# Two eight-expert layers: every expert over every token, or tokens sorted by expert through DRAM

## The chip, the cores and the metric

The kernel runs on one core of one Trainium2 chip. The metric is device time in microseconds (us) of one execution; lower is better. Everything is float32 unless said otherwise.

## The reference, cut to what matters

Sixty-four sequences of 64 tokens, 128 values each, go through twelve residual layers: cross-attentions to a context of 128 tokens a sequence, a gated recurrence, low-rank and four-expert layers, softmax attentions, a convolutional state-space layer. Two of the twelve send each token to one of eight experts, and these are what the change rewrites:

```python
# layer L2 (called m2 in the kernel): x + routed(layernorm(x))
idx = argmax(softmax(x @ Wr + br)); gate = max(softmax(...))
# tokens past an expert's capacity (4096 / 8 = 512, counted over the whole batch) are dropped
h = relu(expert_in @ W1[e] + b1[e]);  out = gate * (h @ W2[e] + b2[e])
# layer L3 (called m3): no gate, no capacity
idx = argmax(softmax(xf @ Wg + bg))
h = gelu(x @ W1[e] + b1[e]);  out = h @ W2[e] + b2[e]     # for e = idx of the token
```

W1[e] and W2[e] are 128 x 128.

## The kernel before

The 64 sequences are worked in four passes. In a pass two slots, 0 and 1, each hold 8 sequences: 512 tokens as four tiles of 128 (`TILES` = 4). One slot in one pass is called a unit here; there are eight. Each slot has its own buffers (X, Z, A, T, big, P, small, ...) and its own four banks of PSUM (`ps_0`, `ps_1`, 512 float32 columns a bank). So a unit goes through all layers as one chain, and the two slots are independent streams that fill each other's gaps on each engine.

For each engine there is a generator `program(s)` that yields between steps ("beats"); `weave` merges the two slots' generators by a bit string in `ORDER` that was written beforehand: one bit a beat says which slot comes next. Each engine then runs its instructions strictly in that order, and an instruction that waits holds back everything behind it on its engine, the other slot's too. There is one such order each for TensorE (pe, 2,498 beats), ScalarE (act), VectorE (dve), GpSimd (pool) and the DMA queue of SyncE (sp). On DVE, `link` puts a semaphore between dependent instructions of one chain.

The stages of a unit, in order, by the names used below: three groups of attention heads (`h0`, `h1`, later `h2`; 44 TensorE beats each, in four pairs j0 to j3), `rnn`, `lora`, `x1` (cross), `lin`, `m1` (softmax attention and the four-expert layer), `h2`, `loc` (softmax attention), `m2`, `x3` (concat), `ssm`, `m3`, then the next pass.

In m2 and m3 every one of the eight experts is computed for all 512 tokens and a mask makes the wrong ones vanish. A unit and layer takes on TensorE:

- `turn_onehot`: four transposes of the one-hot choice; ScalarE copies the rows, scaled so that a wrong expert gets -1e30, into `mTb` (L1212, L1213);
- `up` (L889): 8 matmuls of 512 columns with W1[e]; `mask` (L893): 8 bf16 matmuls of 512 columns that add the -1e30 into the same bank, so that relu or gelu gives 0 for wrong tokens; ScalarE's `hidden` (L1315) evicts with bias and function;
- `down`: 8 x 4 matmuls of 128 columns with W2[e] (recorded at the helper `tokens`, L486), all summed in one bank; `tokens8` (L908): 4 matmuls that add the second bias.
- In m2 also a transpose of the scaled tokens, and `positions`-like matmuls (L921 to L926) that count tokens by expert for the capacity.

A float32 matmul leaves two records in the trace, a transpose or a bf16 matmul one. All weights stay in SBUF (`wts`); the first-layer weights of both expert layers are centred once at the start (`centre_weights`, L693, 9 chunks), which makes the mean subtraction of the layer norm unnecessary.

Of the kernel before, what the change touches and what calls it, by code (L numbers as in the profile page):

```python
# [13 lines left out]
D = 128  # L14
BATCH, SEQ, CTX = 64, 64, 128
SLOTS = 2
# [16 lines left out]
EXPERTS = 8  # L33
CAPACITY = BATCH * SEQ // EXPERTS
# [8 lines left out]
           ("bqkv", 3), ("moe2_b1", 8), ("conv_w", 8), ("conv_b", 2), ("moe3_b1", 8),  # L43
# [4 lines left out]
           ("loc_q", 128), ("loc_k", 128), ("loc_v", 128), ("moe2_r", 8), ("moe2_w1", 1024), ("x3a", 128), ("ssm_in", 512),  # L48
           ("moe3_r", 8), ("moe3_w1", 1024)]
# [5 lines left out]

CONSTS = [("ident", 128), ("center", 128), ("hmask8", 8), ("cos", SEQ), ("sin", SEQ),
          ("causal_add", SEQ), ("causal_T", SEQ), ("upto", 128), ("iota", 16)]


def offsets(table):  # L60
    at, out = 0, {}
    for name, n in table:
# [14 lines left out]
    pe=(2498, int(""  # L77
        "404600c8640004010800000000069ebffdf375f56bac10c1af4ddee629cc55cb06914148810afbdc018a1ca1dd3aea84c3e9"
        "c718588ed73ea800018bfd2ff8eeff53ec40001008e1d720e74051814070f83ff8382011c3a86cb5fd6febfbbc1c3fc3f6be"
        "cccfc9476f7fbd7dee707114148a0a7def5401651c3ac0c754163eb71c58b2c5ae72000031bf767ff15fde3dc4a0c3e0ebb8"  # L80
        "2246bffffc0003902b06a40100000e439f3ff8b6fd6eeffdff647fc30abfa6ee58a2955ed703911029140530ef3d502c48e0"
        "ebaea85bfff7b7be0b144aacd402003e97fd1f15d1f4000129ddea1b801158affffe1a82e00e20000000896b8ff7faeb75f5"
        "ffc1860ae9bffefeffc1f85bf2f38ca502505053d3ced401660e33f2d482affffffffe07ffbdffffeefc192d91eeb2a04181"
        "2dfb1ff19e1d41389fff30f", 16)),
    act=(1741, int(""
        "4120206080200000c00039bbffe4faf4fbbecfa82c43130cc0901c000424af78f68bde1856031e6e0e18fee19bfff5810301"
        "4e974e32054b018c306405ee0ccfddff73fffee99f10e8fbf7be8b0cc090382010ab95a0f687de350c30cdaa00f1fecc9bff"
        "dd21ccbfaed022dbf00068fb40010001773393fdefffde7fefeef1a24256470cc024118020224f0efcd3fffb35f0081ed507"
        "0fa7f80df9800ecf5fc310055f1e58ff000000009cf3e7bbf67ffbb7ff5ff13e03e6e06c0840e02010cb62fe641bffffff5f"
        "ff4ffff5838af0bfd2213de037fa0178ff", 16)),  # L90
    dve=(2030, int(""
        "1001238a8c0040200000001bbf6bbd7c3b15a5ce31825da73db18614c0dbf16c50d0df8007c68ea4daee65bf0c38303288d8"
        "f8abf796e6dedd83ec028a69e0c7641de80000620488fb961e400a5ff9c78fe3e7186a7f643cfffe78f03cfc5b1593fc3b50"
        "11d294e78078efc30e483c818de81af7e6bb6d5be17ffde6e068e5c64002b6561230800007c0206d7baeef7bfc1ff1e25d73"
        "35cc61923a0f3f0e858d060ee1da28cca539dcddf97fa33c066518c2fd7aeee06d941ef377981c01973e306dc5801800000e"
        "370022eddcb9ffc441aa4fffeb5fe9e1ce79e037d928b46fc3e5011e88ce7b1913fbffffe1fffcffffe4f1b19c78c77f000e"
        "b367fd", 16)),
    pool=(610, int(""
        "6c5018df30532b53182161b93a2fbb7378c7904c253ac34fc0ff53185609d43957dee378c7cb219c0e0dee3a2b53142131b5"
        "3af57f8db607c0b9807706bc935fa660ac0ae49ffff3be7d1d", 16)),  # L100
    sp=(26, int(""
        "1333335", 16)))


def weave(program, order):
# [50 lines left out]
def build(nc, x, ctxin, ctok_in, fold, cols, weights, consts, out):  # L156
# [4 lines left out]
    with stack:  # L161
# [113 lines left out]
        def block_of(h, n):  # L275
            return (h % 2) * (n // 2) + h // 2
# [1882 lines left out]
```

## Time and profile before

| | |
|---|---|
| time, median of 3 runs | 2491.32 us (2490.16 to 2494.02) |
| span of the profiled execution (first to last instruction) | 2495.5 us |
| busy share of the span | TensorE 94%, weight loads 63%, VectorE 59%, ScalarE 47%, GpSimd 37% |
| DMA | 26.57 MB, nearly all of it in the first of 40 slices of the span |
| mean granted TensorE clock | 0.989 of full speed |

The span of the one profiled execution is 4.2 us above the median of the runs. PE is TensorE, PEld its weight loads (which overlap with matmuls), DVE VectorE, ACT ScalarE, POOL GpSimd, SP SyncE. L486 is line 486 of the kernel. In a group, "busy" is the time in which at least one of its instructions ran, so that busy divided by the count is the price of one in a packed stream, while the mean of one is longer, since matmuls overlap.

### The profile page before, as it was taken

Reading aid. Unit: us, or ns where it says so; the run is one execution under the profiler, and the core shown is the slowest. Engines: PE = TensorE matmul, PEld = TensorE weight load, DVE = VectorE, ACT = ScalarE, POOL = GpSimd, SP = SyncE. Lnnn points to the kernel's source line nnn. Section 1 sums busy time; section 2 is a strip of 40 time slices with the busy share of each in tenths; the row PEclk is TensorE's granted clock in tenths of the full one; section 3 lists DMA queues with packets and bytes.
Section 4 is the critical chain, followed back from the end, with each engine's and each line's share of the span. In section 5 each row is a group of like instructions: output and inputs, shape, how many; then the busy total and the mean of one; then the engine's idle time right before and its main releaser. Section 6 shows DMA issues by size and latency. Waiting matters only on the chain.

```text
span 2495.5 us, 41931 instructions
## 1 busy us (share of the span) xinstructions
PE 2349.7 (94%) x16426; PEld 1565.0 (63%) x16426; DVE 1479.9 (59%) x4040; ACT 1180.3 (47%) x2996; POOL 929.6 (37%) x853
## 2 busy tenths in 40 slices
PE   9999989999999999999999999999999999999998
PEld 6665656666766665666666665566566666656665
DVE  5357556665475566666564567665565555664653
ACT  5454334455444534545554444445454444354543
POOL 5235343433233335434231344443322343544410
PEclk9999989999999999999999999999999999999999
DMA  5000000000000000000000000000000000000000
GB/s 233 1 1 1 1 10 9 10 1 18 1 1 10 1 1 10 10 9 9 9 1 9 1 1 9 1 10 9 13 1 1 5 1 1 1 1 1 2 1 9
DMA packets 6821, 26.57 MB, mean 11 GB/s; under 512 B 864, under 2 KB 992, under 8 KB 5984
## 3 DMA queue, kind: packets, MB, share of 16 engines
q1 hardware_dynamic: 6624, 23.89, 2.7%
q8 instruction: 130, 2.13, 0.4%
q14 instruction: 67, 0.55, 0.1%
HBM read 21.79 MB, written 2.10 MB: 10 GB/s over the span
## 4 chain that ended last, share of the span: by engine, by line
PE 71%; DVE 18%; POOL 4%; ACT 4%; issue 3%; DMA 0%; DVEq 0%; POOLq 0%; ACTq 0%
PE ps L486 10%; PE ps L499 6%; PE ps L549 6%; PE ps L518 6%; PE ps L889 4%; PE ps L510 3%; PE ps L628 3%; PE ps L471 3%; PE ps L603 3%; PE ps L596 3%; PE ps L650 3%; PE ps L836 2%; PE ps L601 2%; PE ps L846 2%; PE ps L677 2%
## 5 line engine op out<-in xcount | busy, mean ns | idle before, releaser
L1919 POOL TENSOR_TENSOR P<-P,small 128x384 f32<-128x384 f32 x384 | 317.7, 850 | 555.2 <-DVE small L1430 554.8
L1140 ACT ACTIVATE P<-ps,small 128x192 f32<-128x192 f32 x768 | 314.2, 421 | 147.1 <-DVE small L1422 145.6
L1892 POOL TENSOR_TENSOR small<-small,mhalf 128x4 f32<-128x4 f32 x112 | 128.4, 1147 | 543.4 <-DVE small L1410 272.1
L499 PE MATMUL ps<-kvT,big 128*128 128x192 f32 x1536 | 313.8, 334 | 7.2 <-DVE big L1437 2.8
L499 PEld LDWEIGHTS ps<-kvT,big 128*128 128x128 f32 x1536 | 248.2, 190 | 91.2 <-issue 53.5
L1422 DVE TENSOR_REDUCE small<-ps 128x2 f32<-128x384 f32 x384 | 210.1, 551 | 107.7 <-PE ps L499 100.8
L486 PEld LDWEIGHTS ps<-wts,P 128*128 128x128 f32 x1920 | 231.5, 192 | 43.8 <-issue 30.0
L486 PE MATMUL ps<-wts,P 128*128 128x128 f32 x1920 | 249.0, 279 | 5.2 <-POOL P L2009 2.6
L2009 POOL TENSOR_TENSOR P<-T 128x512 f32<-128x512 f32 x96 | 126.6, 1319 | 206.7 <-ACT T L1289 107.6
L518 PEld LDWEIGHTS ps<-value,big 128*128 128x128 f32 x1536 | 178.1, 192 | 26.9 <-issue 20.7
L518 PE MATMUL ps<-value,big 128*128 128x128 f32 x1536 | 188.4, 277 | 0.5 <-DVE big L1462 0.5
L510 PE MATMUL ps<-cst,P 128*128 128x128 f32 x1152 | 167.3, 279 | 18.8 <-POOL P L1919 9.3
L549 PE MATMUL ps<-kvT,score 128*128 128x512 f32 x384 | 177.9, 604 | 4.6 <-ACT kvT L1115 3.5
L510 PEld LDWEIGHTS ps<-cst,P 128*128 128x128 f32 x1152 | 132.7, 143 | 51.1 <-issue 18.2
L1140 ACT ACTIVATION_READ_ACCUMULATOR P<-ps,small 128x1 f32 x768 | 156.8, 204 | 0.0
L1315 ACT ACTIVATE P<-ps,col 128x512 f32<-128x512 f32 x128 | 81.4, 684 | 134.5 <-PE ps L893 134.3
L1488 DVE SCALAR_TENSOR_TENSOR X<-ps,small,X 128x128 f32<-128x128 f32 x256 | 71.9, 343 | 104.4 <-PE ps L486 100.1
L372 POOL TENSOR_TENSOR big<-big,cst 128x1024 f32<-128x1024 f32 x48 | 106.6, 2222 | 66.1 <-ACT big L1307 37.8
L628 PEld LDWEIGHTS ps<-Vbd,P 128*64 128x64 f32 x3072 | 99.0, 139 | 51.1 <-issue 34.4
L1627 DVE TENSOR_REDUCE small<-ps 128x8 f32<-128x512 f32 x128 | 87.7, 685 | 59.3 <-PE ps L650 59.1
L1157 ACT ACTIVATE big<-ps 128x512 f32<-128x512 f32 x96 | 57.3, 596 | 135.1 <-PE ps L510 134.7
L549 PEld LDWEIGHTS ps<-kvT,score 128*128 128x128 f32 x384 | 69.5, 192 | 81.3 <-issue 72.6
(288 smaller groups left out, 4483.5 us busy)
## 6 DMA issues: line engine op xcount, KB each, us to landing
ctok<-ctok_dram SPq DMA_DIRECT2D x8, 512.0 KB, 3.7
ctxT<-ctx_dram SPq DMA_DIRECT2D x8, 512.0 KB, 3.9
wts<-weights_dram SPq DMA_DIRECT2D x1, 2530.0 KB, 23.7
wts<-weights_dram SPq DMA_DIRECT2D x1, 2189.0 KB, 18.1
X<-x_dram SPq DMA_DIRECT2D x8, 256.0 KB, 3.0
big<-fold_dram SPq DMA_DIRECT2D x2, 1024.0 KB, 7.9
out_dram<-X SPq DMA_DIRECT2D x8, 256.0 KB, 2.0
wts<-weights_dram SPq DMA_DIRECT2D x1, 1536.0 KB, 26.1
```

What stands on the lines that cost most here:

```text
L372: return engine.tensor_tensor(big[s][:, 1024 * (t % 2):1024 * (t % 2) + 1024].rearrange("p (b j t) -> p b j t", b=2, t=SEQ), src[:, 128 * ...
L486: m = pe.matmul(part(s, k, t), tile_of(src, t), w, start=first and t == 0 and c == 0, stop=last and t == TILES - 1 and c == len(pairs) - 1)
L499: m = pe.matmul(ps[s][:, at:at + KEYS], big[s][:, BANK * b + 128 * p:BANK * b + 128 * p + 128], kvT[s][:, keys_at(b):keys_at(b) + KEYS], s ...
L510: m = pe.transpose(part(s, k, p), probs(s, j)[:, PAIR * p + at:PAIR * p + at + 128], C("ident"))
L518: m = pe.matmul(part(s, 1, t), big[s][:, 1024 * t + 128 * k:1024 * t + 128 * k + 128], value[:, at:at + 128], start=(t == 0 and k == 0), s ...
L549: m = pe.matmul(bank(s, qp_bank(g, r) + k), score[:, 128 * block_of(h, nh):128 * block_of(h, nh) + 128], latents(s), start=True, stop=True)
L628: m = pe.matmul(ps[s][64 * bb:64 * bb + 64, at:at + 18], src(bb, j), Vbd[s][:, 18 * (8 * b + j):18 * (8 * b + j) + 18], start=True, stop=True)
L1140: m = act.activation(probs(s, b // 2)[:, to:to + KEYS], ps[s][:, at:at + KEYS], ACT.Exp, bias=small[s][:, 4 * e + p:4 * e + p + 1], accum_ ...
L1422: dve.tensor_reduce(small[s][:, at:at + 2], ps[s][:, BANK * k:BANK * k + 2 * KEYS].rearrange("p (c k) -> p c k", k=KEYS), AX.X, ALU.max, n ...
L1892: pool.tensor_tensor(rstd(s, name, n), variance(s, name, n), mhalf[:, 0:n], ALU.pow).then_inc(*sig("rstd", s))
L1919: m = pool.tensor_tensor(view, view, over(small[s][:, at:at + 2], 2, [128, 2, KEYS]), ALU.mult)
L2009: pool.tensor_tensor(P[s][:, 1024 + 512 * (k % 2):1536 + 512 * (k % 2)], tmp(s, k % 2), tmp(s, 2 + k % 2), ALU.mult)\
```

## The change

In both layers the 512 tokens of a unit are sorted by expert and each expert works on its own tokens only.

1. DVE's new `places` computes from the counts, for each token, a row in a table of 11 tiles of 128 rows (`ROUTED` = 4 + 8 - 1; each expert's tokens begin on a new tile), and for each of the 11 tiles its expert (`which`). m3 now makes the same counting matmuls as m2.
2. GpSimd scatters the tokens by four indirect DMAs (one for 128 rows of 512 bytes) to `x_sorted` in DRAM. SyncE's queue reads the 11 expert numbers into a register one by one, loads for each tile its expert's weights (128 x 385 float32: W1, W2, b2 broadcast, b1; 197 KB) from a table in DRAM, and then reads the sorted tokens in three DMAs, for groups of 4, 4 and 3 tiles.
3. TensorE transposes 11 tiles, ACT copies them, TensorE makes 11 `up` matmuls of 128 columns, ACT evicts 11 times 128 columns with bias and function, TensorE makes 11 `down` matmuls, DVE adds b2 group by group.
4. SyncE writes the three groups to `y_sorted` in DRAM, GpSimd gathers back by four indirect DMAs, DVE adds to the residual.

The expert weights leave `wts`, so their centring goes as well (9 chunks become 5), and DVE's `centre` is put in for m2 and m3. At the start SyncE also fills `x_sorted` with two copies in DRAM. Semaphores that both slots shared (`ONCE`) become one per slot, mostly on the counters of a stream (`tok`, `zT`, `n_proj`, `pl`), at the same waits. The orders are new: pe has 2,294 beats.

```diff
+                def routed(s, i, layer):                     # SyncE
+                    for g, (first, tiles) in enumerate(GROUPS):
+                        yield
+                        sp.wait_ge(*on("tok", s, i, ROUTES[layer] + ".e"))
+                        for k in range(first, first + tiles):
+                            e = sp.value_load(which[s][0:1, k:k + 1], min_val=0, max_val=128 * (EXPERTS - 1))
+                            sp.dma_start(expert(s, k), table[layer][bass.ds(e, 128), :]).then_inc(experts_in[s][g], 16)
+                    yield
+                    sp.wait_ge(moved[s], 128 * n + 64)
+                    for g in range(3):
+                        sp.dma_start(by_tile(sorted_x(s, g)), rows_in(x_sorted[s], g)).then_inc(sorted_in[s][g], 16)
+                    for g in range(3):
+                        yield
+                        sp.wait_ge(*on("tok", s, i, f"{ROUTES[layer]}.y{g}"))
+                        sp.dma_start(rows_in(y_sorted[s], g), by_tile(sorted_y(s, g))).then_inc(sorted_out[s], 16)
...
-                def up(s, layer, e, src, first):
-                def mask(s, e, first):
-                def down(s, i, layer, e):
...
+                def routed(s, i, layer):                     # TensorE
+                    def turn_x(g):
+                        pe.wait_ge(sorted_in[s][g], 16 * n + 16)
...
+                    def up(g):
+                        pe.wait_ge(experts_in[s][g], 16 * tiles * (n + 1))
+                        pe.wait_ge(*on("zT", s, i, f"{ROUTES[layer]}.t{g}"))
...
+                            m = pe.matmul(part(s, U_BANK[g], k), expert(s, first + k)[:, 0:128], tile_of(sorted_xT(s, g), k),
+                                          start=True, stop=True)
...
+                    yield from turn_x(0)
+                    yield from turn_x(1)
+                    yield from up(0)
+                    yield from turn_x(2)
+                    yield from up(1)
+                    yield from down(0)
+                    yield from up(2)
+                    yield from down(1)
+                    yield from down(2)
...
+                def places(s):                               # VectorE, 11 steps, 7 of them before "which" is out
...
+                def scatter(s, i, layer):                    # GpSimd
+                    pool.wait_ge(*on("tok", s, i, ROUTES[layer] + ".d"))
+                    for t in range(TILES):
+                        pool.indirect_dma_start(x_sorted[s], bass.IndirectOffsetOnAxis(ap=dest[s][:, t:t + 1], axis=0), tile_of(N[s], t), None)\
+                            .then_inc(moved[s], 16)
+                def gather(s, i, layer):
+                    pool.wait_ge(sorted_out[s], 48 * (2 * i + layer) + 48)
...
+                    dve.wait_ge(moved[s], 128 * (2 * i) + 128)
```

## Rows read from the trace of the kernel before

**Rows 1.** The page: busy time by engine, and granted clock in 40 slices
```profile
PE 2349.7 (94%) x16426; PEld 1565.0 (63%) x16426; DVE 1479.9 (59%) x4040; ACT 1180.3 (47%) x2996; POOL 929.6 (37%) x853
...
PEclk9999989999999999999999999999999999999999
```

**Rows 2.** Waits of TensorE: waited for, us in total, times, longest
```profile
PE ps L471 <- DVE P L1405: 31.1, 42, 2.9
```

**Rows 3.** The page: the chain that ended last, by engine
```profile
PE 71%; DVE 18%; POOL 4%; ACT 4%; issue 3%; DMA 0%; DVEq 0%; POOLq 0%; ACTq 0%
```

**Rows 4.** Groups by line, TensorE: busy us, mean ns, idle before them
```profile
L486 PE MATMUL ps<-wts,P 128*128 128x128 f32 x1920 | 249.0, 279 | 5.2 <-POOL P L2009 2.6 <-DVE P L1827 1.9 <-DVE X L1488 0.5
...
L510 PE MATMUL ps<-cst,P 128*128 128x128 f32 x1152 | 167.3, 279 | 18.8 <-POOL P L1919 9.3 <-ACT big L1157 3.1 <-issue 1.9
...
L889 PE MATMUL ps<-Z,wts 128*128 128x512 f32 x128 | 64.6, 629 | 0.3 <-ACT P L1315 0.3
L889 PE MATMUL ps<-A,wts 128*128 128x512 f32 x128 | 62.2, 609 | 2.3 <-ACT P L1315 1.3 <-ACT A L1115 0.9
L471 PE MATMUL ps<-cst,P 128*128 128x128 f32 x352 | 58.6, 291 | 35.8 <-DVE P L1405 31.1 <-DVE P L1782 4.5
...
L893 PE MATMUL ps<-mTb,pick_b 8*128 8x512 bf16 x128 | 24.6, 384 | 0.9 <-ACT T L1213 0.9
...
L908 PE MATMUL ps<-wts,T 8*128 8x128 f32 x128 | 17.0, 271 | 0.0
...
L478 PE MATMUL ps<-cst,small 128*8 128x128 f32 x64 | 10.1, 283 | 0.0
...
L693 PE MATMUL ps<-wts,cst 128*128 128x512 f32 (+1 forms) x18 | 7.7, 571 | 0.0
...
L923 PE MATMUL ps<-ohb,upto_b 128*128 128x8 bf16 x32 | 3.2, 168 | 0.5 <-DVE ohb L1768 0.5
```

**Rows 5.** Stretches: length, busy PE, PEld, DVE, ACT, POOL, clock, DMA share, GB/s
```profile
10.00:20.00 10.00, 9.90 (x61) 5.65 (x60) 5.65 (x16) 3.42 (x7) 6.27 (x4) 1.00 1.04 422
...
70.00:120.00 50.00, 49.08 (x244) 32.33 (x243) 19.51 (x38) 24.96 (x83) 15.04 (x18) 1.00 0.00 1
...
590.00:600.00 10.00, 7.77 (x47) 4.86 (x47) 6.16 (x13) 6.47 (x22) 6.95 (x6) 0.83 0.00 0
2340.00:2370.00 30.00, 26.04 (x348) 18.27 (x347) 22.67 (x47) 15.80 (x29) 8.82 (x5) 1.00 0.01 2
2376.00:2496.00 120.00, 104.52 (x648) 68.81 (x648) 51.71 (x196) 44.55 (x73) 9.89 (x14) 0.97 0.02 5
2432.00:2448.00 16.00, 9.71 (x48) 5.77 (x48) 12.45 (x34) 5.27 (x8) 3.85 (x6) 1.00 0.00 1
```

**Rows 6.** Timeline of VectorE in m2, last pass: start, length
```profile
2381.70 0.19 DVE L1778 SCALAR_TENSOR_TENSOR small<-small 128x32 f32<-128x32 f32 x1
```

**Rows 7.** Groups by line, ScalarE
```profile
L1315 ACT ACTIVATE P<-ps,col 128x512 f32<-128x512 f32 x128 | 81.4, 684 | 134.5 <-PE ps L893 134.3
...
L1115 ACT ACTIVATE Z<-ps 128x512 f32<-128x512 f32 x72 | 43.0, 598 | 50.5 <-PE ps L471 50.2
...
L1263 ACT ACTIVATE P<-ps,small 128x128 f32<-128x128 f32 x32 | 11.3, 367 | 7.3 <-DVE small L1593 7.2
```

**Rows 8.** Groups by line, GpSimd
```profile
L1892 POOL TENSOR_TENSOR small<-small,mhalf 128x4 f32<-128x4 f32 x112 | 128.4, 1147 | 543.4 <-DVE small L1410 272.1 <-DVE small L1512 167.6 <-DVE small L1728 36.3
...
L372 POOL TENSOR_TENSOR big<-big,cst 128x1024 f32<-128x1024 f32 x48 | 106.6, 2222 | 66.1 <-ACT big L1307 37.8 <-PE ps L650 25.3 <-DVE big L1682 2.5
```

**Rows 9.** DMA issues: size of one, median us to landing
```profile
X<-x_dram SPq DMA_DIRECT2D x8, 256.0 KB, 3.0
...
out_dram<-X SPq DMA_DIRECT2D x8, 256.0 KB, 2.0
```

**Rows 10.** Groups by line, VectorE: two instructions of one shape
```profile
L1405 DVE TENSOR_TENSOR P<-X,small 128x512 f32<-128x512 f32 x48 | 48.4, 1009 | 21.3 <-POOL small L1892 21.0
...
L1782 DVE TENSOR_TENSOR P<-X,small 128x512 f32<-128x512 f32 x8 | 5.5, 692 | 0.3
```

More of the change, by code:

```diff
@@ L445, in _ @@
                     sp.dma_start(wts[:, cut[k]:cut[k + 1]], weights[:, cut[k]:cut[k + 1]]).then_inc(w_main, 16)
+                for s in range(SLOTS):
+                    sp.dma_start(x_sorted[s].rearrange("(k p) d -> p k d", p=128), by_tile(x[:, 0:128 * ROUTED])).then_inc(filled, 16)
                 weave(program, ORDER["sp"])
@@ L1553, in top2_weights, with routed @@
+                def routed(s, i, layer):
+                    for g in range(3):
+                        yield
+                        dve.wait_ge(*on("y_ps", s, i, f"{ROUTES[layer]}.y{g}"))
+                        dve.tensor_tensor(by_tile(sorted_y(s, g)), by_tile(bank(s, D_BANK[g])[:, 0:128 * GROUPS[g][1]]), expert_b2(s, g),
+                                          ALU.add).then_inc(*sig("tok", s))
                 def top2_weights(s, i, name, e):
@@ L1785, in moe2 @@
                         yield from contexts(s, i)
+                    yield from routed(s, i, 0)
                     yield
-                    dve.wait_ge(*on("y_ps", s, i, "m2"))
-                    link(add_scaled(s, i, 2, lambda t: small[s][:, DN + 12 + t:DN + 13 + t]))
+                    dve.wait_ge(moved[s], 128 * (2 * i) + 128)
+                    for t in range(TILES):
+                        at = small[s][:, DN + 12 + t:DN + 13 + t]
+                        m = dve.scalar_tensor_tensor(tile_of(res(s, i), t), tile_of(N[s], t), at, tile_of(res(s, i), t), ALU.mult, ALU.add)
+                    link(m)
                 def concat(s, i):
@@ L1937, in kv_context @@
                     if i >= 0:
[L1938 removed]
+                        pool.wait_ge(*on("tok", s, i, "ssm.g"))
                     else:
@@ L2028, in program @@
                         yield from inverse_root(s, i, "m2")
+                        yield from scatter(s, i, 0)
                         if i < PASSES - 1:
@@ L2031, in program @@
                             yield from inverse_root(s, i, "ctx1")
+                        yield from gather(s, i, 0)
                         yield from inverse_root(s, i, "x3")
@@ L2043, in program @@
                             yield from inverse_root(s, i, "x0")
+                        yield from gather(s, i, 1)
+                        if i < PASSES - 1:
                             yield from kv_latents(s, i)
@@ L2067, in rows_of @@
         return w.reshape(n, 128, -1).transpose(1, 0, 2).reshape(128, -1)
-    def at(p, a):
-        out = np.zeros((128, a.shape[-1]), np.float32)
-        out[:p] = a
-        return out
     def per_partition(v, n):
```

510 lines of the change are left out of this document (275 added, 235 removed), and 2 rows, old and new, of the table WEIGHTS.

## The prediction, as it was put on record

> **What bounds the kernel now.** I read the page first: TensorE is busy for 2349.7 us of a span of 2495.5 us, in every slice of it, at a granted clock of 0.9 and more of 2.4 GHz [rows 1]. So 145.8 us are all the idle time that TensorE has. The chain that ended last agrees: 71% of it is TensorE, and no DMA is in it [rows 3]. Then the waits: the largest for which TensorE stood is a transpose behind a layer norm, 31.1 us in 42 times, never over 2.9 us [rows 2]. No engine is waited for long; the two slots fill each other's gaps. Hence two questions decide: how much TensorE work goes, and how much idle time comes in because a unit now waits in each expert layer for DMAs that take work of no engine.
>
> **What TensorE loses and gains** (eight units, two layers each; a float32 matmul is two records). Prices are busy time by count [rows 4].
> - Removed: `up` 64.6 + 62.2 = 126.8 us; `mask` 24.6; `down` 8 x 4 x 2 x 16 = 1024 of the 1920 records of L486 at 249.0 / 1920 = 0.130 us, 132.8; the bias matmuls L908 17.0; the one-hot transposes L478 10.1; the token transpose of m2, 32 of the 352 of L471 at 0.166, 5.3. Sum 316.6 us.
> - Added: 11 x 16 = 176 transposes at 167.3 / 1152 = 0.145 us, 25.5; `up` 11 x 2 x 16 = 352 records of 128 columns at 0.130, 45.7; `down` the same, 45.7; in m3 14 counting matmuls of 8 columns a unit, 112 at 3.2 / 32 = 0.10, 11.2. Sum 128.1 us.
> - Centring: 18 records become 10, 8/18 of 7.7 us = 3.4 us less.
>
> Net -191.9 us: TensorE 2349.7 - 191.9 = 2157.8 us. With the idle time of today that is 2303.6 us of span. I take the group prices as they are, since weight loads overlap in the new matmuls as in L486's.
>
> **The other engines** don't become the bound. ACT loses 81.4 us (L1315) and six small copies a unit, and gains 176 evictions of 128 columns at 0.367 us = 65 us and 48 copies at up to 0.6 = 29 us [rows 7]: about even. DVE gains, per unit, two `places` of 11 steps at 0.2 us [rows 6], six additions of up to 0.69 us and two centrings of 0.7 to 1.0 us [rows 10], some 10 us, 80 in all: 1560 us, two thirds of the new span. POOL gains 16 x 8 = 128 indirect DMAs: at 1.1 to 2.2 us (below) 140 to 280 us of its queue beside 930 busy us. The semaphores per slot stand at the same waits as the shared ones, and the instructions behind them are the same: 0. The two fills of `x_sorted` at the start are behind all weights in SP's queue and run while TensorE works: 0; if they were in the way, 0.7 MB each at 422 GB/s [rows 5] is under 4 us. 2.2 MB less of weights could give a few us back only where the start waits for them, and it doesn't: 0.
>
> **The two DMA legs.** The trace of before has no indirect DMA, no register load from SBUF and no wait on DRAM inside a pass. Bounds for one unit and layer:
> - First leg, from the counting matmuls to the first transpose of sorted tokens. `places` 11 x 0.21 = 2.3 us. Four scatters on POOL's queue, each between 1.1 us (its cheapest work on data, four columns) and 2.2 us (its 1024 columns) [rows 8]; I take 1.1, since a scatter handles one number a row: 4.4. Landing 2.0 and reading back 3.0 us, as a store and a load of 256 KB [rows 9]. Sum 11.7 us, with 2.2 us each 16.1. Beside it SP loads 11 experts, 2.17 MB, 5.1 us at 422 GB/s [rows 5], and reads 11 numbers first, which may cost 0 or up to 1.1 us each; the three reads of tokens stand behind all of this in the same queue. From `which`, 1.6 us in, at 11 x 0.8 = 9 us and the reads of 3, plus some of the data still under way: 14 to 17. I take 16 us for the leg.
> - Second leg: last b2 addition 0.5, store 2.0, four gathers 4.4, landing 2.5, additions to the residual 1.4 (four of 0.34): 10.8, at 2.2 us a gather 15. I take 12 us.
> - Between them the experts' own chain (transposes, copy, `up`, evictions, `down`) is 6 to 8 us.
>
> Who covers a leg? The bits of the new pe order can be decoded by counting beats. Slot 0 in m2 waits behind slot 1's h2: 2 projections, 4 score beats and 8 beats of j0 (two passes), or 15 beats (one): 13 to 16 us of TensorE work. One slot alone in such heads keeps TensorE at 98%: from 70 to 120 us slot 0's h1 runs with hardly any work of slot 1, and PE is busy 49.08 of 50 us [rows 5]. The second leg of m2 has 16 beats of heads, 17 us. There the legs cost nothing. Weak covers:
> - Last pass. From slot 0's count in m2 on, today's end is 2376 to 2496: 120 us, PE busy 104.5, idle 15.5 [rows 5]. Four expert layers lie there, each 191.9 / 16 = 12 us lighter; 11 beats of loc (some 15 us) move in as cover: 104.5 - 48 + 15 = 71 us of work. The new chain of slot 1: 24 us behind slot 0, leg 16, experts 6, leg 12, x3 and ssm to m3's logits 38 (as in today's), routing 4, leg 16, experts 8, leg 12, add 1: 137 us. Idle 66, so +50 us.
> - Slot 0's m3 stands behind 10 beats of loc in two passes and 5 in the third; a stretch of such work has PE at 26.04 of 30 us [rows 5]: 3 + 3 + 8 = 14 us. Its second leg has some 8 us of cover for 12, three times, since the next pass's h0 waits for the residual: +12. Slot 1 in the first pass has 6 beats of rnn and lora (PE at 9.71 of 16 in a comparable stretch [rows 5]: +6) and then 3 beats of x1: +7. Together +39, say 40.
> - Where the cover is 13.4 us and the leg 16, five or six times: +15.
>
> Added idle 105 us. Sum: 2303.6 + 105 = 2408.6 us of span; the median of runs lies 4.2 us under today's span, so **2404 us**. Today's PE-only idle after a wait already drops the clock (590 to 600: 2.2 us idle, clock 0.83 [rows 5]); longer gaps could cost some us more in the tail, and I let the bounds hold that.
>
> **A rule that speaks against this change.** In today's trace two VectorE instructions of one shape take 692 ns in one place and 1009 ns on average in another [rows 10], so something holds DVE up beside POOL's work. The Trainium skill, "SBUF — State Buffer", section "Who interferes with whom", says that a VectorE copy or tensor_scalar in a two-port mode fully blocks GpSimd's descriptor writing, and names a software DMA that took 620 ns alone and about 3100 ns beside a copy. By that rule a scatter or gather that meets such an instruction would be some 2.5 us later, and all eight of a layer 20 us later at worst. It is the mechanism of the third rival. The skill's "DMA: Bandwidth & Descriptors", section on the anatomy of a SWDGE DMA, gives 2.0 us plus bytes / 436e3 for one: 2.15 us for 64 KB, as an estimate, and with it the legs would be as above.
>
> **Rivals.**
> 1. Everything but the tail is hidden, because the order was laid for legs of just this length: 2303.6 + 50 - 4.2 = 2349 us. For it: today's waits are all under 3 us [rows 2]. Against: the covers of 5 loc beats and of 3 x1 beats are too thin by count. Chance 0.15.
> 2. The legs are 3 to 5 us longer a layer than I have them (gathers at 2.2 us, reads behind 11 loads). In an order fixed beforehand TensorE stands for each: 16 x 3 to 16 x 5, so 2452 to 2484 us. Chance 0.10.
> 3. The other side: POOL's queue or SP's is far dearer, 10 us a layer. TensorE stands at the sorted tokens, and the gather, in order in POOL's queue, holds back the other slot's normalising (L1919), for which its transposes wait. 2404 + 160 = 2564 us. It decides from (2496 - 2404) / 16 = 5.8 us a layer on. For it: nothing in the trace bounds an indirect DMA or 11 register loads from above. Against: 5.8 us a layer is 0.7 us on every one of eight indirect DMAs beyond 1.1, with all slack gone. Chance 0.16.
> 4. The cut buys nothing because the units' chains, not TensorE, set the time: gain and loss cancel within 5 us. At 94% busy that needs 190 us of new idle time. Chance 0.04.
>
> My forecast has 0.55, with a range of its own of 2350 to 2450 us.
>
> **How the numbers follow.** 0.2% of this time, 5 us, is about what a measurement can tell from no change. Faster: forecast, rivals 1 and 2, 0.80; same 0.04; slower 0.16. The range leaves out rival 3 and a little below rival 1: 2325 to 2495 us holds about 0.8.
>
> **What would show it.** PE busy near 2158 us, L889's and L893's groups gone, two new groups of 352 records near 46 us each: the sum is right. Waits of TensorE for sorted tokens (a DMA) few and under 5 us, except in the last 140 us and at slot 0's m3: the covers are right. TensorE waits of 6 us and more in every layer, on a DMA or behind L1919, would make the prediction wrong upwards; a last stretch shorter than 137 us, downwards. PE busy well over 2158 us would mean that the prices of records, or the clock, are not today's.

## The result, and the profile after

The changed kernel took 2553.4 us (median of 4 runs, 2543.2 to 2556.6) against 2492.7 us before in the same session: ratio 1.0231, 95% interval 1.0204 to 1.0258. It is 61 us slower: the forecast of 2404 us and its range of 2325 to 2495 us were wrong, and so was the sign.

The page of the changed kernel: span, busy time by engine, granted clock, the chain that ended last.

```profile
span 2554.8 us, 42262 instructions
...
PE 2247.1 (88%) x15778; PEld 1542.7 (60%) x15778; DVE 1560.1 (61%) x4270; ACT 1126.7 (44%) x3032; POOL 1048.8 (41%) x981
...
PEclk9999999988989998998899999999699999999866
...
PE 61%; DVE 20%; issue 5%; SPq 5%; POOL 4%; ACT 4%; DMA 3%; POOLq 0%; DVEq 0%; ACTq 0%
```

Against [rows 1] TensorE lost 103 us of busy time, where 192 were forecast, and its idle time went from 146 to 308 us, where 251 were forecast. The clock shows 8, and once 6, where a pass is in its expert layers (one 8, at 960 to 1020 us, lies outside them), and 6 at the end. TensorE's share of the chain that ended last fell from 71% [rows 3] to 61%, and SyncE's queue (SPq) and DMAs are now in it. (The kernel before read its data less early than the table ahead of the prediction says: its first slice moved 233 GB/s for 62 us, some 14.5 of the 26.57 MB. The DMAs were in no wait of note there.) Waits of TensorE (us in total, times, longest):

```profile
PE ps L531 <- DVE P L1450: 46.4, 36, 4.6
PE ps L960 <- DMA P<-x_sorted: 32.7, 18, 7.2
PE ps L944 <- DVE ohb L1592: 29.4, 12, 8.0
PE ps L538 <- DVE big L1547: 17.0, 7, 5.5
```

The first is the wait of [rows 2], grown from 31.1 us. The new waits for sorted tokens (a DMA) are just 33 us; those on VectorE grew more. All waits together are 290 us against 137, 189 of them on VectorE against 90. The groups that the forecast had priced (busy, mean ns, idle before):

```profile
L960 PE MATMUL ps<-cst,P 128*128 128x128 f32 x176 | 35.6, 338 | 32.9 <-DMA P<-x_sorted 32.7
L971 PE MATMUL ps<-Z,big 128*128 128x128 f32 x128 | 22.3, 331 | 1.8 <-ACT Z L1351 1.8
L971 PE MATMUL ps<-A,big 128*128 128x128 f32 x128 | 18.4, 291 | 0.0
L971 PE MATMUL ps<-T,held 128*128 128x128 f32 x96 | 13.3, 275 | 0.0
```

The transposes cost 35.6 us (forecast 25.5), `up` 22.3 + 18.4 + 13.3 = 54.0 (forecast 45.7): 40% and 18% over the forecast. Work that nobody touched got dearer too: the matmuls of the scores (L601 here, L549 in the kernel before) take 191.0 us, where the same 384 records took 177.9.

Where the time lies is seen in stretches that begin when slot 0's counting matmuls run in m2 (length, busy PE, PEld, DVE, ACT, POOL, clock, DMA share, GB/s). The changed kernel: its first stretch of expert layers, the stretch behind it, and the last one:

```profile
472.00:764.00 292.00, 241.39 (x1454) 169.50 (x1456) 178.81 (x519) 126.89 (x358) 116.64 (x118) 0.89 0.22 63
764.00:1100.00 336.00, 318.46 (x2442) 214.46 (x2442) 212.72 (x539) 152.35 (x396) 145.62 (x123) 0.96 0.02 5
...
2388.00:2555.00 167.00, 94.47 (x628) 69.30 (x628) 80.14 (x268) 43.62 (x97) 45.47 (x47) 0.68 0.37 105
```

The kernel before, its first stretch of expert layers:

```profile
470.00:760.00 290.00, 274.69 (x1682) 185.80 (x1681) 169.06 (x487) 146.32 (x366) 97.55 (x96) 0.99 0.02 6
```

TensorE is busy 33 us less there, and the stretch is 2 us longer. The last stretch grew from 120 us [rows 5] to 167, at a clock of 0.68. Below is one layer's first leg as it stands on the chain that ended last (start, length in us), from the last step of `places` ahead of `which` to the first transpose, with the eleven expert loads between.

```profile
602.69 0.18 DVE which L1618
602.89 0.28 SPq L440
603.19 0.15 SPq L440
603.60 0.36 SPq L441
604.01 0.27 SPq L440
...
615.02 0.34 SPq L441
615.41 0.43 SPq L445
615.88 4.09 DMA P<-x_sorted
620.02 1.11 PE ps L960 x4
```

A register load of an expert's number (L440) and its DMA's issue (L441) repeat every 1.13 us, 12.5 us for eleven, and the reads of the tokens (L445) stand behind them. From the one-hot choice at 600.17 (the counting matmuls follow at 600.4) to 620.02 the leg is 20 us, where 16 were forecast. GpSimd was done with the last of the four scatters at 611.5, 3.9 us before the reads were issued.

### The profile page after: what moved, and what is told of

It reads as the page before. It is cut to its first block, busy times and chain, and to the rows that moved or that the text cites. A ratio compares the mean times of both kernels' runs of the same rounds, so it can differ in the third digit from the quotient of the medians.

```text
span 2554.8 us, 42262 instructions
## 1 busy us (share of the span) xinstructions
PE 2247.1 (88%) x15778; PEld 1542.7 (60%) x15778; DVE 1560.1 (61%) x4270; ACT 1126.7 (44%) x3032; POOL 1048.8 (41%) x981
## 4 chain that ended last, share of the span: by engine, by line
PE 61%; DVE 20%; issue 5%; SPq 5%; POOL 4%; ACT 4%; DMA 3%; POOLq 0%; DVEq 0%; ACTq 0%
PE ps L551 7%; PE ps L570 6%; PE ps L538 5%; PE ps L601 4%; PE ps L562 4%; PE ps L680 3%; PE ps L655 3%; PE ps L898 3%; PE ps L653 3%; PE ps L648 3%; PE ps L531 2%; PE ps L888 2%; SPq L440 2%; DVE small L1435 2%; PE ps L702 2%
## 5 line engine op out<-in xcount | busy, mean ns | idle before, releaser
L601 PE MATMUL ps<-kvT,score 128*128 128x512 f32 x384 | 191.0, 641 | 3.3 <-DVE big L1482 1.7
L538 PEld LDWEIGHTS ps<-wts,P 128*128 128x128 f32 x896 | 117.0, 199 | 44.3 <-issue 27.0
L680 PEld LDWEIGHTS ps<-Vbd,P 128*64 128x64 f32 x3072 | 105.5, 146 | 55.7 <-issue 34.0
L538 PE MATMUL ps<-wts,P 128*128 128x128 f32 x896 | 124.0, 286 | 8.1 <-DVE P L1909 6.3
L601 PEld LDWEIGHTS ps<-kvT,score 128*128 128x128 f32 x384 | 74.7, 206 | 87.5 <-issue 79.6
L680 PE MATMUL ps<-Vbd,P 128*64 128x18 f32 x3072 | 115.9, 218 | 3.2 <-DVE P L1732 2.0
L1159 ACT ACTIVATE Z<-ps 128x512 f32<-128x512 f32 x72 | 43.0, 597 | 152.7 <-PE ps L531 152.5
L1325 ACT ACTIVATE T<-ps 128x512 f32<-128x512 f32 x96 | 57.3, 597 | 119.9 <-PE ps L898 119.7
```

What stands on the lines that cost most here:

```text
L538: m = pe.matmul(part(s, k, t), tile_of(src, t), w, start=first and t == 0 and c == 0, stop=last and t == TILES - 1 and c == len(pairs) - 1)
L601: m = pe.matmul(bank(s, qp_bank(g, r) + k), score[:, 128 * block_of(h, nh):128 * block_of(h, nh) + 128], latents(s), start=True, stop=True)
L680: m = pe.matmul(ps[s][64 * bb:64 * bb + 64, at:at + 18], src(bb, j), Vbd[s][:, 18 * (8 * b + j):18 * (8 * b + j) + 18], start=True, stop=True)
```

## The experiments

The kernel before was run beside each; a ratio is of the runs of one session. x1, s1 and r1 are variants of the kernel before, all others of the changed one. The variants without register loads, those without scatters and gathers, e9 and x1 leave work out, as said at each, and so their output is not the reference's. s1 and s2 change the order alone and don't give the reference's output either; why isn't known, so they are used for their lengths only. Each of the three s runs ran only twice.

```
kernel                                               us     ratio   95% interval
the change                                         2553.4  1.0231  1.0204-1.0258
e1  no register loads                              2525.7  1.0127  1.0096-1.0157
e2  e1, three weight DMAs a layer                  2525.5  1.0133  1.0108-1.0158
e3  no scatters, no gathers                        2541.1  1.0201  1.0173-1.0230
e5  token reads after four expert loads            2537.2  1.0186  1.0148-1.0224
e7  e2 and e3                                      2488.1  0.9983  0.9968-0.9997
n1  e7, token reads ahead of the weights           2484.2  0.9965  0.9942-0.9988
x2  n1, no reads and no stores either              2483.7  0.9966  0.9954-0.9978
x1  the kernel before, 195 us of TensorE cut       2441.9  0.9804  0.9787-0.9822
e4  TensorE filler ahead of two waits a layer      2576.3  1.0350  1.0318-1.0382
e8  expert matmuls twice                           2624.4  1.0509  1.0481-1.0537
e9  places in two constant steps                   2552.0  1.0218  1.0190-1.0245
s1  before, slots apart                            3633.9  1.4560  1.4527-1.4594
s2  the change, slots apart                        3913.2  1.5680  1.5635-1.5724
s3  e7, slots apart                                3659.9  1.4665  1.4630-1.4699
p1  e7 in another order                            2516.7  1.0087  1.0065-1.0109
n2  n1 in another order                            2466.0  0.9882  0.9862-0.9903
r1  before in another order                        2491.6  0.9993  0.9980-1.0005
r2  e5 in another order                            2533.6  1.0152  1.0134-1.0171
```

### The legs: SyncE's queue and the indirect DMAs

e1 takes fixed experts, so nothing is read into registers:

```diff
-e = sp.value_load(which[s][0:1, k:k + 1], min_val=0, max_val=128 * (EXPERTS - 1))
-sp.dma_start(expert(s, k), table[layer][bass.ds(e, 128), :])...
+e = 128 * min(k, EXPERTS - 1)
+sp.dma_start(expert(s, k), table[layer][e:e + 128, :])...
```

> The changed kernel with the 11 expert numbers not read into a register: tile k always loads expert min(k, 7), so most tokens meet a wrong expert; all DMAs keep their size and place. Theory A (SyncE's queue is what the first leg waits for: in the trace of the changed kernel one register load and one DMA issue take 1.13 us together, 11 of them 12.4 us, and the reads of the sorted tokens stand behind them): one load falls to about 0.4 us, the leg shortens by 8 us, of which 5 to 8 reach TensorE in each of 16 layers: 2430 to 2475 us. Theory B (the loss is TensorE's own: gaps behind the router's chain on VectorE, and the clock at half after each gap): only the gaps at the sorted tokens go, 2515 to 2540 us. Theory C (the indirect DMAs on GpSimd and their landing are what is waited for): no change, 2545 to 2560 us.

e2 also loads each group's experts with one DMA:

```diff
-for k in range(first, first + tiles):
-    ... sp.dma_start(expert(s, k), ...)
+e0 = 128 * min(first, EXPERTS - tiles)
+sp.dma_start(held_in..., table[layer][e0:e0 + 128 * tiles, :].rearrange("(k p) c -> p k c", p=128))...
```

> As e1_static, but the weights of a group of tiles come in one DMA, three a layer in place of 11, of the same bytes; the experts are fixed as there. Theory A: the queue work before the reads falls from 12.4 us to some 1.5; the scatter and its landing (9 us after the expert numbers are out) then end the leg, so at most a few us below e1_static, 2400 to 2465 us. If the bytes of the weights (2.17 MB a layer) and not their issue hold the reads back, then equal to the changed kernel, 2545 to 2560 us. Theory B: 2515 to 2540 us. Theory C: 2545 to 2560 us.

e3 leaves out the scatters and gathers (L2046, L2053) on GpSimd:

```diff
-sp.wait_ge(moved[s], 128 * n + 64)
+sp.wait_ge(filled, 32)
+sp.wait_ge(*on("tok", s, i, ROUTES[layer] + ".d"))
...
-dve.wait_ge(moved[s], 128 * (2 * i) + 128)
+dve.wait_ge(sorted_out[s], 96 * i + 48)
```

> The changed kernel without its 128 indirect DMAs: SyncE reads what the start put into the sorted table, VectorE waits for the store of the sorted results and adds its own unsorted tokens; the output leaves the routing out. Register loads, weight loads, reads and stores stay. Theory C: both legs lose their GpSimd part, 4 to 9 us each, 2400 to 2450 us. Theory A: the first leg is SyncE's and stays; only the second shortens by some 6 us, where its cover was thin: 2500 to 2540 us. Theory B: 2530 to 2555 us.

e5 moves the reads up in SyncE's queue:

```diff
 for g, (first, tiles) in enumerate(GROUPS):
+    if g == 1:
+        yield
+        read_tokens(s, n)
     yield
```

> The changed kernel, computing the same, with one edit on SyncE's queue: the three reads of the sorted tokens stand behind the first four weight loads and ahead of the other seven. Theory A (SyncE's queue): the tokens can be there some 14 us after the expert numbers in place of 17 to 19, the weights of groups 1 and 2 some 3 us later than now but still ahead of their matmuls; e1_static, which took 8 us off the queue in each layer, brought 28 us, so some 10 to 15 us: 2535 to 2545 us. Theory D (the two units' own chains and the fixed order set the time, and every leg is only one term): the same range, it doesn't tell them apart. If the reads wait for the scatter at the head of the queue longer than they save: 2555 to 2565 us.

e7 is e2 and e3 together:

> e2_grouped and e3_no_indirect together: no register loads, three weight loads a layer, no indirect DMA; SyncE's reads and stores are all that is left of the legs (some 5 and 3 us in place of 20 and 11). Output without routing. Theory A with C (the legs are the whole loss): 25 us a layer less in the chain, TensorE near its sum of 2158 us plus 150 to 200 us idle: 2330 to 2400 us. Theory D (legs are a part; the rest is the router's chain and places on VectorE, with too little TensorE work left to hide them): 2450 to 2490 us. Theory B (clock): it falls with the gaps, so between.

The register loads are worth 26 us (1.0231 to 1.0127), fewer DMAs nothing more. Theory A expected 78 us and more of e1, so most of the loss isn't there. Reordering the queue, which keeps the function, gets back 11 us, and taking out the indirect DMAs alone 7 us; for these two the intervals overlap with that of the change. On top of e2, taking them out is worth 37 us (1.0133 to 0.9983). That is how two parallel ways of one leg behave: the register loads beside the scatters hide them, and only the longer way counts until it is cut. POOL's two groups in the changed kernel say what one costs:

```profile
L2046 POOL DMA_INDIRECT x_sorted<-P,dest x64 | 65.7, 1026 | 82.1 <-DVE P L1860 44.3 <-DVE dest L1621 22.3 <-issue 15.5
L2053 POOL DMA_INDIRECT P<-y_sorted,dest x64 | 63.7, 995 | 112.0 <-DMA y_sorted<-P 96.7 <-issue 15.3
```

About 1.0 us each, 1.3 with the gap to the next: the forecast's 1.1. Yet with both ways gone e7 stands only 4 us under the kernel before, not 190. In e7 the reads still waited behind 2.2 MB of weights:

```profile
P<-x_sorted SPq DMA_DIRECT2D x32, 256.0 KB, 7.5
```

n1 puts them first (as e5, at `g == 0`); x2 leaves out every way of the tokens through DRAM, the reads and the stores of sorted rows as well:

```diff
-pe.wait_ge(sorted_in[s][g], 16 * n + 16)
+pe.wait_ge(*on("tok", s, i, ROUTES[layer] + ".d"))
```

> The changed kernel without scatters and gathers and with grouped weight loads at fixed experts, as the run at 2488 us, but its three reads of tokens stand ahead of the weight loads in SyncE's queue (tokens are not moved: output is not the reference's). In that run laid apart TensorE still waited 178 us for these reads, 11 us a layer, which landed 7.5 us after their issue behind 2.1 MB of weights. Theory E (a slot's own chain sets the time, the other slot covers most of it): 4 to 6 us less a layer in the chain, of which a quarter reaches the time: 2460 to 2475 us. Rival F (only the written order is wrong, the chain is covered): 2488 us, no change.

> The changed kernel with all ways of the tokens through DRAM taken out of the layer: no scatters, no reads, no stores of the sorted rows, no gathers, and expert weights loaded in three DMAs from fixed experts (TensorE transposes whatever stands in the buffer: output is not the reference's). Places, counting matmuls, copies, additions and the written order stay. Theory H (what still costs 180 us against the sum is the tokens' way out and back): 2350 to 2400 us. Theory G (the order's gaps and the clock, not the DRAM, hold it): 2460 to 2484 us.

Neither moved much: 0.9965 and 0.9966 against e7's 0.9983, with intervals that overlap. n1 stayed above the range of theory E, x2 fell into that of theory G. So all that the legs cost is the way from x2 to the change, 0.9966 to 1.0231, 66 us. And the changed kernel without any leg is within 9 us of the kernel before. In x2 TensorE is busy for 2225.8 us of 2480.2, so it idles for 254 us, 109 more than before the change, though no leg is left, and it is busy for 68 us more than the 2157.8 us of the sum. That refutes the view that the legs ate the gain. Something else had.

### Does cut TensorE work come back?

x1 makes only the cut, in the kernel before: experts 1 to 6 lose their `up` and `down` matmuls, and the masks (which now open their bank's sum), ScalarE's evictions, the waits and the order stay.

```diff
 def up(s, layer, e, src, first):
+    if e not in (0, EXPERTS - 1):
+        return None
...
 def down(s, i, layer, e):
...
+    if e not in (0, EXPERTS - 1):
+        return
```

> The kernel before, with only TensorE's expert work cut: of the eight experts only numbers 0 and 7 keep their up and down matmuls (output is not the reference's); masks, evictions on ScalarE, VectorE's work, waits and order are all kept. That takes 6/8 of 126.8 + 132.8 us, 194.7 us of TensorE's work, as much as my sum gave the whole change, and adds nothing. Theory H (cut TensorE work comes back one for one while the other slot fills its gaps, as the prediction's sum has it): about 2300 us. Theory G (the dense expert matmuls were what filled TensorE while the other slot waited; without them its gaps open and its clock falls): 2380 to 2440 us, waits of TensorE near 220 us.

This is the run that decides: a cut of 195 us, with nothing added, gave 50 us (ratio 0.9804), at the edge of theory G's range. Its page, and its waits of TensorE:

```profile
PE 2232.0 (92%) x15466; PEld 1475.1 (60%) x15466; DVE 1477.4 (61%) x4040; ACT 1178.9 (48%) x2996; POOL 929.3 (38%) x853
...
PEclk9999989998999999989999999999999999999986
```

```profile
PE ps L471 <- DVE P L1409: 44.8, 45, 4.2
PE ps L486 <- ACT P L1319: 13.3, 9, 1.7
PE ps L891 <- ACT P L1319: 11.5, 10, 2.8
```

```profile
L486 PE MATMUL ps<-wts,P 128*128 128x128 f32 x1152 | 165.7, 291 | 19.2 <-ACT P L1319 13.3 <-DVE P L1831 2.7 <-POOL P L2013 2.6
```

TensorE's busy time fell by 118 us, not by 195. In the two groups that were cut, L486 lost 768 records and 83.3 us, not 99.8, and L891 (L889 before) lost 80.6 us, not 95.1: 31 us less together, for the records that stayed cost more than their group's mean had been. The rest of TensorE's busy time, where no work was taken out, grew by 46 us (164 - 118): 33 us in the other groups themselves, the masks among them, and 13 because groups overlap less. A large part of this is the clock, which is 0.95 in the first expert stretch. An estimate: busy time times granted clock, added up over stretches of 4 us of the trace, gives the work at full clock, 2325 us before and 2158 in x1. By it the cut was worth 167 us of work, and the lower clock took back 50 of them.

And idle time rose by 61 us, from 146 to 207. TensorE reaches the eviction of the hidden rows (L1319), or the other slot's layer norm (the wait of [rows 2], 31.1 to 44.8 us), sooner, and stands there. The dense expert matmuls had hardly waited for anybody (2.6 us of idle time before L889 in [rows 4]), so they are what had filled TensorE while VectorE and ScalarE worked. 195 - 31 - 46 - 61 = 57 us, close to the fall of the span, 56 us.

Two limits of this run have to be said. It keeps all of ScalarE's evictions, for which TensorE now waits 28 us (1.7 before, at L1315), while the change has smaller ones; without those 28 us the cut would still have given back less than half. And no run tells the other slot's wait from the slot's own within the 61 us. x1's first expert stretch and its end, to be read beside the rows above and [rows 5]:

```profile
468.00:740.00 272.00, 240.26 (x1422) 160.13 (x1421) 168.43 (x492) 143.19 (x358) 97.51 (x96) 0.95 0.02 7
...
2332.00:2440.00 108.00, 80.38 (x397) 46.65 (x396) 51.62 (x195) 43.59 (x71) 8.72 (x13) 0.72 0.02 6
```

From the other side, e8 runs each of the 22 expert matmuls of a layer twice, and e4 adds 24 bf16 matmuls a layer ahead of two waits:

```diff
-for k in range(tiles):
+for k in [k for k in range(tiles) for _ in range(2)]:          (e8, up and down)
...
+keep_clock(bank(s, 3), 12)                                     (e4, in m3 and at g == 0 bank 0)
 pe.wait_ge(*on("tok", s, i, "m2.oh"))
```

> The changed kernel with each of the 22 expert matmuls of a layer made twice into the same place: 704 records more, 91 us of TensorE work at 0.13 us each, put exactly where the change took work away. If TensorE's work still sets the time: 2553 + 75 to 91 = 2628 to 2644 us. Theory D (in the expert layers the chains set the time and TensorE has idle time to give): the two copies lengthen each chain by some 5.7 us of which part is hidden, less the clock that is gained: 2560 to 2600 us.

> The changed kernel with 12 matmuls of 512 bf16 columns on constants (2.3 us at full clock) ahead of the counting matmuls' wait and 12 ahead of the first wait for sorted tokens, in every layer: 32 times 2.3 us = 74 us of added TensorE work, placed where TensorE mostly idles. Theory B: idle time is filled, the clock stays at its upper level (mean 0.97 and more in place of 0.934) and the 89 us that TensorE is busy beyond the sum mostly go: 2480 to 2530 us. Theory A: the waits end when SyncE's queue says so, and the clock is a small part: 2545 to 2575 us. If the places don't idle at all: 2553 + up to 74 us.

e8's matmuls, forecast at 91 us, made TensorE busy for 78 us more and the kernel 71 us slower, just under the 2628 us from which TensorE's work alone would set the time and above theory D's range. So in the middle of a slot's chain adding costs nearly in full, while cutting in the kernel before gives a quarter. One account of both is that the added matmuls stand behind each other in the slot's own chain while idle time elsewhere stays (308 us before them, 302 with them); it isn't tested. e4 raised the mean clock of the profiled run from 0.934 to 0.956 and cut the waits from 290 to 247 us, and was 23 us slower: filler matmuls raise the granted clock, and here cost more than that gave back. e9 tests whether the small VectorE steps of `places` set the time:

```diff
 def places(s):
-    ...                                                         (eleven steps)
+    dve.tensor_scalar(which[s][:, :], C("iota")[:, 0:ROUTED], float(EXPERTS - 1), 128.0, ALU.min, ALU.mult)...
+    return dve.tensor_scalar(dest[s][:, :], fixed[:, 0:TILES], 1.0, None, ALU.mult)
```

> The changed kernel with places reduced from 11 dependent steps on VectorE to 2 that copy constants: each token goes to a fixed distinct row, tile k to expert min(k, 7). All DMAs, register loads and matmuls stay. It takes 9 x 0.2 = 1.8 us off VectorE and off the first leg in each layer, 29 us in all, and off what the other slot's softmax waits for behind it in VectorE's queue. Theory D: most of it reaches the time, 2520 to 2535 us. Theories A and C alone: the first leg shortens as much, but the other slot gains nothing, 2535 to 2550 us.

It took 2552.0 us, no change, so they don't.

### A slot's own chain: the slots laid apart

Only the `ORDER` strings change (`-pe=(2294, int("" "a1432e...` to another string of the same length, and so for each engine): each engine takes slot 1's beats only where slot 0 has none, so the total is near the sum of the slots' own chains.

> The kernel before with only its interleaving changed: the same beats of work, but each engine takes a beat of slot 1 only where no beat of slot 0 can go on (one shared count still alternates once a pass), so that the two slots hardly overlap and the total is the sum of two slots' own chains. It is the base for the next run. Theory E (the change lengthened each slot's own chain of dependent work, which the other slot must cover): about 3340 us. Rival F (the chains are as long as before, only the written order fits worse) says nothing else here; both take this as the base.

> The changed kernel with its slots laid apart in the same way. Theory E: its total is longer than that of the kernel before laid apart by some 20 us for each of the 16 routed layers (2 layers, 4 passes, 2 slots), 320 us, 3660 us in all, since a layer's own chain now holds two legs through DRAM of 20 and 12 us against the 12 us of TensorE work that it lost. Rival F: the routed layer's chain is not longer on the whole (legs paid by the shorter expert work), total within 60 us of the base; then the order alone explains the loss.

> The changed kernel with grouped weight loads at fixed experts and with no indirect DMAs (tokens are not moved: output is not the reference's), slots laid apart. Theory E: the legs account for most of the added chain; without them the total is some 100 us above the base (3440 us), 6 us a layer, for the places, the copies through DRAM and the groups. Rival F: no difference from the base beyond 60 us, as the run before it.

All ran 220 to 290 us over the expected level, but the differences answer in part: the change is 279 us longer, 17.5 us for each of 16 routed layers, near theory E's 20, and without indirect DMAs and register loads 26 us, not the 100 of theory E. TensorE is busy 158 us less in s3 than in s1 (2592.6 against 2750.6 us) and waits 180 us more, and its waits for the token reads there, which come in behind the weights, are 178 us. So with what it adds the changed layer is no shorter in a slot's own chain; that the cut alone would shorten it isn't excluded, since no run lays x2 apart. Laid apart, TensorE waits like this (s2):

```profile
PE ps L531 <- DVE P L1450: 314.1, 71, 5.4
PE ps L960 <- DMA P<-x_sorted: 293.5, 19, 28.4
```

That is 18 us a layer for the token reads, of which the kernel as it runs shows 32.7 / 16 = 2: the other slot covers nine tenths of this wait.

### The written order

p1, n2, r1 and r2 change the `ORDER` strings alone, to orders found by a search of list schedules with the traces' durations.

> The changed kernel without the legs (as the run of grouped loads and no indirect DMAs, 2488 us; its output is not the reference's) under another written order on all five engines, found by a search of list schedules with the durations and waits of the traces; beats and waits are the same, only which slot's beat an engine takes first differs. Theory F (the order left standing was laid for legs, and hides the gain): about 2435 us, 50 us below 2488. Theory E (the two chains and their meeting set the time, no order gets it back): 2480 to 2490.

> The kernel of the run before this one (no scatters or gathers, reads ahead, fixed experts; output not the reference's) under another interleaving of the same beats on all engines, from a search of list schedules with the traces' durations and waits. Rival F (the order hid the gain): 2430 to 2445 us, 40 us and more below its sister. Theory E (any order meets the two chains' length): within 15 us of its sister.

> The kernel before, unchanged but for the interleaving of its beats, found by the same search. If such an order gains 40 us and more here too (2450 us and below), the order is worth as much to the kernel before, and is no part of what the routed layers cost. If the order of before was good and only the changed kernel's is poor (rival F), this stays at 2480 to 2500 us.

> The whole changed kernel with its token reads after the first four expert loads (2537 us before), under an interleaving found by the same search. Rival F: 2495 to 2510 us, which is still not below the kernel before. Theory E: 2525 to 2545 us.

p1 lost 29 us against e7, and TensorE waited 66 us for the token reads in it (6.5 in e7). Against their sisters n2 gained 18 us, r2 4 (8 by the ratios; the intervals overlap), r1 nothing. This is one search, and its forecasts for p1, n2 and r2 missed by more than it gained; it says that at least 18 us of order were left in the leg-less kernel, not that no better order exists. The original two-slot order under the new program, or the new order under the old one, wasn't tried: their beats differ.

## Why the prediction was wrong

Split each time where slot 0 counts for the last time in m2 (marks good to 4 us):

```
                       up to the last m2     from there     whole span
before                      2376                120            2496
x1 (the cut alone)          2332                107            2439
x2 (change, no legs)        2332                148            2480
the change                  2388                167            2555
```

- **TensorE 2349.7 - 191.9 with the idle time of today, 2303.6 us: the step that failed.** In the changed kernel itself the 146 us between 2408.6 us of span and 2554.8 are 89 us by which TensorE is busy beyond 2157.8, and 57 us of idle time beyond the 251 forecast. By x1 a cut of that size is worth 50 us, not 192; if that carries over to the changed kernel, 142 of the 149 us between 2404 and 2553 lie in this step, and the added 105 us of idle time were near what the additions cost. "The two slots fill each other's gaps" was right, and its consequence was missed: the work to be cut was the filling. A busy share of 94% was read as a bound by TensorE. Laid apart (s1) the same work has TensorE wait 874 us; that it waits 137 us in [rows 2]'s run is owed to the other slot's work, and the cut took from that. Rival 4, where cut work buys next to nothing, came nearest to this and had 0.04; it wanted 190 us of new idle time, while in x1 61 us of idle time and 77 us of dearer work on TensorE were enough.
- **The prices of records.** "I take the group prices as they are": 31 us too dear for what went (x1), some 20 us too cheap for what came (L960 +10, `up` +8, `down` 49.6 against 45.7). The prediction had named this sign itself: busy time well over 2158 us means that prices or clock are not today's.
- **The clock.** The forecast let its bounds hold "some us more in the tail". It was in every expert stretch. By the estimate above (busy time times granted clock) the changed kernel's work is 2130 us at full clock, 195 less than before, where 192 were forecast; 93 us more than before are the lower clock. So the sum of work was right, the two errors of price nearly cancelled, and by this estimate TensorE's 89 us too many are the clock. Short windows of the changed kernel (columns as above) show the half level, 1.2 GHz, behind windows in which TensorE was busy 0.51 and 1.06 of 4 us, and full speed behind one in which it was busy throughout:

```profile
560.00:564.00 4.00, 0.51 (x14) 0.41 (x14) 3.72 (x15) 0.63 (x1) 0.35 (x2) 0.60 0.00 0
564.00:568.00 4.00, 3.07 (x14) 1.47 (x15) 1.75 (x4) 0.63 (x2) 3.09 (x4) 0.50 0.61 174
...
596.00:600.00 4.00, 1.06 (x8) 0.97 (x8) 2.83 (x19) 2.00 (x3) 2.88 (x3) 0.79 0.12 33
600.00:604.00 4.00, 3.58 (x18) 1.89 (x19) 3.55 (x19) 0.00 (x0) 0.00 (x0) 0.50 0.00 0
...
636.00:640.00 4.00, 4.00 (x21) 2.22 (x20) 2.27 (x6) 1.85 (x6) 3.22 (x4) 1.00 0.22 66
640.00:644.00 4.00, 4.00 (x26) 3.48 (x25) 2.17 (x5) 3.36 (x14) 0.77 (x1) 1.00 0.12 36
```

- **Weak covers +40 and cover 13.4 against 16 +15.** 55 us ahead of the tail; from x2 to the change it is 2388 - 2332 = 56. The size was right, perhaps by luck. That it came from the covers counted there isn't shown: the leg was 20 us, not 16, since a register load and issue cost 1.13 us (0 to 1.1 forecast for the load, 0.8 taken for both), and most of the time shows as waits on VectorE.
- **Last stretch 137 us.** It was 167. Without legs it is already 148, where x1 has 107: slot 1's counting comes 40 us behind slot 0's (x2; 36 in the change), not 24, and TensorE is busy 97 of 148 us at a clock of 0.69. Of the 41 us between x1 and x2, the larger distance of the slots (15 to 40 us) makes 25, slot 1's own chain (90 to 105 us from its count to the end) 15, and the rest lies in the marks. At the very end slot 0's stores of sorted rows stand in SyncE's queue behind slot 1's eleven loads and three reads: the first rows were ready at 2525.6, and their store was issued at 2530.6.
- **Indirect DMAs 1.1 us, second leg 12 us.** Right: 1.03 and 1.00 us, and 13.2 us from the last b2 addition (642.05) to the end of the additions to the residual (655.22) in the layer looked at.
- **DVE contending with POOL's descriptors.** The Trainium skill ("SBUF — State Buffer", "Who interferes with whom") lets a VectorE copy in a two-port mode block a software DMA; an estimate from the page's 620 and 3100 ns, which stand in its section "A bandwidth-pool intuition that's wrong (but worth ruling out)", is some 2.5 us. The 128 indirect DMAs here took 1.0 us in the mean on GpSimd. The twelve that ran beside a VectorE copy took 0.95 to 1.09 us, but these copies (L1499, L1507) read from PSUM; in this trace no copy within SBUF ran beside one, so no run here shows the rule or speaks against it. The longest, 2.00 us, ran beside VectorE work on two SBUF operands (L1543).
- **Rival 3** named 2564 us, near the 2553 measured, but by luck: the legs together cost 66 us, 4 us a layer, under the 5.8 from which it was to decide. The slowdown needed the cut's failure too.
- **What is not settled.** Why the changed kernel without legs needs the same 2332 us up to the tail as x1, though VectorE has 77 us more to do, and which part of the tail's 41 us an order could get back (n2's gain lies ahead of its tail, which is 148 us from slot 0's count against 142 in n1). Also why e8 pays nearly in full for added matmuls where x1 gets back a quarter.

No version that keeps the function beat the kernel before; r1 equals it, and the best whole variant of the change, r2, is 1.5% slower.

## What to carry to other kernels

Before work is cut from the busiest engine, ask who waits beside it: with two interleaved streams, a stretch of matmuls that wait for nobody can be the cover of other engines' short steps, and only what is left of the cut after that cover, and after a lower clock, counts. Test it as x1 does, by leaving the work out of the old kernel; that one run tells roughly what the cut can bring before anything is built. And price a leg by its longest parallel way: here eleven register loads and issues in SyncE's queue ahead of the reads hid the indirect DMAs that looked dangerous.

## What the runs showed of the hardware

- A number loaded from SBUF into a register on SyncE with the DMA that uses it took 1.13 us (0.28 + 0.15 for the load, 0.34 to 0.36 for the issue, the rest between them); without the 176 register loads the kernel took 26 us less (e1).
- An indirect DMA of 128 rows of 512 bytes took 1.0 us on GpSimd, and the next followed after 0.3 us.
- The same 384 matmuls (L549 before, L601 after) took 177.9 us before (mean clock 0.989), 191.0 in the changed kernel (0.934) and 210.4 in it with the slots apart (0.778).
- Reads of 256 KB took 3.8 us behind eleven single loads and 7.5 us behind three grouped ones of the same 2.2 MB (e7), medians from issue to landing.
